# Attention scores as three float32r terms in four 32-row quarters, quartered masks, grouped silus and a new written order

## The reference, cut to what matters

```python
xn = _layernorm(x)                                   # x: 4 batches, 1024 tokens, 128 channels
q, k, v = split(xn @ Wqkv)                           # 16 heads of 8
scores = einsum("bhqd,bhkd->bhqk", rope(Q), rope(K)) / sqrt(8)
attn = softmax(where(causal, scores, min))
y = (attn @ V) @ Wproj
mlp = (silu(xn @ Wg + bg) * (xn @ Wu + bu)) @ Wd + bd
# experts: 4 heads, sums of two lists of top 8 of 64 keys, the best 8 of the sums, softmax of them;
# weight = silu(xn . down_embed[i]) * softmax; states = sum of weight * up_embed[i] over 512 experts
return x + y + mlp + states
```

## Time and profile before

| | us |
|---|---|
| median of 3 runs (lowest, highest) | 736.49 (734.74, 736.72) |
| span of the profiled execution | 737.5 |
| PE busy | 658.8 |
| DVE busy | 591.9 |
| ACT busy | 539.6 |
| POOL busy | 446.4 |

### The profile page before, as it was taken

How to read it: one execution, slowest core, us unless ns; L and a number is a source line. 1 busy time by engine, 2 the same in 40 slices (tenths; PEclk the granted TensorE clock), 3 DMA queues, 4 the chain that set the end, 5 groups by cost and what they waited for, 6 DMA issues and landing times. The chain is left out here.

```text
span 737.5 us, 15130 instructions
## 1 busy us (share of the span) xinstructions
PE 658.8 (89%) x5628; PEld 268.0 (36%) x5628; DVE 591.9 (80%) x1204; ACT 539.6 (73%) x833; POOL 446.4 (61%) x652
## 2 busy tenths in 40 slices
PE   3977787779999989999999979999998999999996
PEld 2433233223334433333234434433333333344343
DVE  4549898999989999896976898877999898855451
ACT  3333455777878676899887686788689999888882
...
GB/s 145 103 127 49 73 36 24 47 14 3 2 14 20 54 74 61 15 71 20 1 10 21 17 80 63 21 76 13 2 14 31 4 14 1 16 32 16 8 15 38
DMA packets 36566, 26.67 MB, mean 36 GB/s; under 512 B 7084, under 2 KB 34092, under 8 KB 36492
## 3 DMA queue, kind: packets, MB, share of 16 engines
...
...
## 5 line engine op out<-in xcount | busy, mean ns | idle before, releaser
L1159 DVE TENSOR_REDUCE pmax<-banks 128x2 f32<-128x1024 f32 (+3 forms) x304 | 342.2, 1160 | 55.6 <-PE banks L1331 36.3
L1006 ACT ACTIVATE pT<-banks 128x1024 f32<-128x1024 f32 (+3 forms) x384 | 295.8, 810 | 74.1 <-PE banks L1359 54.7
L1373 PE MATMUL ybank<-pT,vaug 128*32 128x512 f32 (+3 forms) x1536 | 164.7, 512 | 2.0 <-ACT pT L1006 1.3
L870 POOL TENSOR_TENSOR ssum<-sim 128x512 f32<-128x512 f32 x128 | 145.6, 1143 | 22.9 <-DVE wsum L1206 18.8
L1350 PE MATMUL banks<-qs,ks 51*128 51x512 bf16 (+3 forms) x768 | 123.2, 336 | 22.8 <-ACT pT L1006 14.1
L1321 PE MATMUL banks<-ks,qs 48*128 48x512 bf16 (+3 forms) x768 | 113.4, 337 | 25.5 <-DVE pmax L1159 16.2
L1206 DVE SCALAR_TENSOR_TENSOR wsum<-ssum,best,wsum 128x512 f32<-128x512 f32 x128 | 125.2, 992 | 11.8 <-ACT wsum L1052 11.7
L1052 ACT ACTIVATE wsum<-ssum,wbias 128x512 f32<-128x512 f32 x128 | 90.3, 723 | 24.4 <-POOL ssum L870 22.2
L887 POOL TENSOR_TENSOR coef<-coef,wsum 128x512 f32<-128x512 f32 x64 | 85.4, 1334 | 20.9 <-DVE wsum L1206 20.5
L1350 PEld LDWEIGHTS banks<-qs,ks 51*128 51x128 bf16 x768 | 36.8, 94 | 133.0 <-ACT pT L1006 78.3
L1321 PEld LDWEIGHTS banks<-ks,qs 48*128 48x128 bf16 x768 | 33.1, 94 | 121.6 <-DVE pmax L1159 62.3
...
## 6 DMA issues: line engine op xcount, KB each, us to landing
...
```

Source lines behind the costliest of these rows:

```text
L870: g.tensor_tensor(ssum[:, m % NSS, :, :], s[:, h, 0:XI].unsqueeze(2).to_broadcast([P, XI, NKEYS]), s[:, RH + h:RH + h + 1, :].to_broadcast ...
L1006: a_.activation(pT[:, q % NPT, 2 * e:2 * e + 2, q0:CHUNK], pair(("sc", *n))[:, :, q0:CHUNK], ACT.Exp, scale=SCALE).then_inc(out_sem, 1)
L1159: v.tensor_reduce(pmax[:, c, i % TPC, k0 // CHUNK, js[0] // PP, :, js[0] % PP:js[-1] % PP + 1], pair(("mx", b, c, k))[:, :, 0:wd_ * len(js ...
L1373: ins = t_.matmul(ybank[32 * j:32 * j + 32, q0:CHUNK], vaug[:, b % 2, kt, v0:v0 + 32], pT[:, q % NPT, j, q0:CHUNK], start=kt == 0, stop=kt ...
```

## The change

- **Parts.** A score is now a product in float32r of two parts: `high` (a copy on ACT as float32r, `c0`) and the rest in float32 (`r1` on POOL, `v1` on DVE), which goes into `tAB[:, s, 1, :]`. `c1`, `p2` and `v2` are gone. Three terms remain, so 24 rows a head (26 with the maximum, which has two parts; `n1` has two POOL instructions in place of four). `high` and `tAB` are read by the row DMAs, so `rp` of a unit now waits until the rows of the unit two before have landed, where it waited for `p2` or `v2`.
- **Quarters.** Four heads lie in four 32-row quarters of the array, named by `tile_position`. A score task takes two quarters, and its last number says which two (rows 0 to 63 or 64 to 127). The number of score tasks and of score products is the same.
- **Masks** take four steps of 32 rows (128, 96, 64 and 32 columns for each block in `mx`, 32 to 128 in `sc`) in place of two, still in bf16. The small products grow from 704 to 1408 in `mx` and from 1024 to 2048 in `sc`.
- **Pairs.** "+" in `PE_ORDER` issues two score tasks together, both products first and then their masks in turn. There are 71 such pairs, all of opposite halves, 59 of them of two diagonal tasks; 55 stand behind the last value product of batch 0.
- **DMAs.** The row DMAs are as many as before (12 a unit) with rows of 2 KB in place of 1 KB; those of the maxima go from 32 to 64, those of the rows of ones from 4 to 8.
- **Order.** All five strings are new. The silus of gate and down product of a chunk stand together on ACT, and expert work of the first stages stands further ahead. In the second half of batch 0 the four gate products of its second chunk (`gt.0.1.*`) hold the banks 2 to 5 while 25 score tasks in a row go through the pair 01.

```diff
 TPC = CHUNK // P
 NF = F // P
-PAIRS = H // 2
-GROUPS = H // 4
+ROWS = 32
+NE = P // ROWS
+GROUPS = H // NE
...
-PP = PAIRS // PARTS
-
-TERMS = [(0, 0), (0, 1), (1, 0), (0, 2), (1, 1), (2, 0)]
+PP = GROUPS // PARTS
+
+TERMS = [(0, 0), (0, 1), (1, 0)]
 KQ = len(TERMS) * DH
-KE = KQ + 3
+KE = KQ + 2
...
-            units += [(i, k0, w, range(j, j + n)) for j in range(0, PAIRS, n)]
+            units += [(i, k0, w, range(j, j + n), half) for j in range(0, GROUPS, n) for half in range(2)]
     return sorted(units, key=lambda u: u[3][0] // PP)
...
 
-    order, place = [], {}
+    order, place, partner = [], {}, {}
     for word in text.split():
...
+        together = []
+        for part in word.split("+"):
+            name, _, slot = part.partition("@")
+            kind, *rest = name.split(".")
+            task = (kind, *(int(r) for r in rest))
+            together.append(task)
+            if slot:
+                place[task] = [int(k) for k in slot]
+        order += together
+        if len(together) == 2:
+            partner[together[0]] = together[1]
+    return order, place, partner
...
-qk.0.1.1@45 gt.0.0.3@5 gt.0.0.0@4 up.0.0.1@1 up.0.0.0@4 up.0.0.3@0 xt.1@12 up.0.0.2@6 dn.0.0.2@5 mx.0.0.0@01
+qk.0.1.1@23 dn.0.0.3@6 dn.0.0.0@0 dn.0.0.1@4 vm.1@56 qk.1.0.0@01 mx.0.0.0@23 mx.0.0.1@45 ac.0.0.0@6 mx.0.0.2@23
+sc.3.0.2.3.0@23 sc.3.0.3.0.1@01 pv.3.0.2.2 pv.3.0.2.3 sc.3.0.3.1.1@23+sc.3.0.3.0.0@45 sc.3.0.3.1.0@01 sc.3.0.3.2.0@45
...
 
         ident = sb("ident", [P, P])
-        identb = sb("identb", [P, P], BF16)
-
-        id2 = sb("id2", [P, 2, P], BF16)
-        mask2 = sb("mask2", [P, 2, 1, P], BF16)
-        maskT2 = sb("maskT2", [P, 2, P], BF16)
+
+        shifted = sb("shifted", [P, 2 * P - ROWS], BF16)
+        mask = sb("mask", [P, 1, P], BF16)
+        maskT = sb("maskT", [P, P], BF16)
...
-        parts = sb("parts", [P, 2, 3, CHUNK], BF16)
-        qs = sb("qs", [P, NQS, PAIRS, CHUNK], BF16)
-        ks = sb("ks", [P, 2, PAIRS, T], BF16)
+        high = sb("high", [P, 2, CHUNK], F32R)
+        qs = sb("qs", [P, NQS, GROUPS, CHUNK], F32R)
+        ks = sb("ks", [P, 2, GROUPS, T], F32R)
         VW = (H - 1) * (DH + 1) + 32
...
-                        for hh in range(2 if m > 0 else 1):
-                            r = HALF * hh + DH * t
+                        for e in range(NE if m > 0 else NE // 2):
+                            r = ROWS * e + DH * t
                             dst = ks[r:r + DH, b % 2, :, cols] if a else qs[r:r + DH, m % NQS, :, :]
-                            sp.dma_start(dst, parts[HALF * hh:HALF * (hh + 1), u % 2, term[a], :])\
+                            src = high[:, u % 2, :].bitcast(F32) if term[a] == 0 else tAB[:, u % 2, 1, :]
+                            sp.dma_start(dst.bitcast(F32), src[ROWS * e:ROWS * (e + 1), :])\
                                 .then_inc(rows_loaded[u % 2], 16)
...
-                    g.tensor_tensor(tAB[:, s, 0, :], tAB[:, s, 0, :], parts[:, s, 0, :], ALU.subtract)\
-                        .then_inc(out_sem, 1)
-                elif kind == "p2":
-                    b, c, a = n
-                    s = unit(b, c, a) % 2
-                    w.wait_ge(done["r1"], rank("r1", b, c, a))
-                    w.wait_ge(done["c1"], rank("c1", b, c, a))
-                    g.tensor_tensor(parts[:, s, 2, :], tAB[:, s, 0, :], parts[:, s, 1, :], ALU.subtract)\
+                    g.tensor_tensor(tAB[:, s, 1, :], tAB[:, s, 0, :], high[:, s, :].bitcast(F32), ALU.subtract)\
...
-                    k = mark(g.tensor_tensor(m, m, nparts[:, c, :, h, :, 0, :], ALU.subtract))
-                    need(k)
-                    k = mark(g.tensor_copy(nparts[:, c, :, h, :, 1, :], m))
-                    need(k)
-                    g.tensor_tensor(nparts[:, c, :, h, :, 2, :], m, nparts[:, c, :, h, :, 1, :], ALU.subtract)\
-                        .then_inc(out_sem, 1)
+                    g.tensor_tensor(nparts[:, c, :, h, :, 1, :], m, nparts[:, c, :, h, :, 0, :].bitcast(F32),
+                                    ALU.subtract).then_inc(out_sem, 1)
...
-                    elif u < 2:
-                        w.wait_ge(done["v1"], rank("v1", b, c, a))
-                    else:
-                        w.wait_ge(done["r1"], rank("r1", b, c, a))
-                    a_.activation(parts[:, s, int(kind == "c1"), :], tAB[:, s, 0, :], ACT.Copy).then_inc(out_sem, 1)
+                        w.wait_ge(rows_loaded[a], rows(*unit_at(u - 2)))
+                    a_.activation(high[:, s, :], tAB[:, s, 0, :], ACT.Copy).then_inc(out_sem, 1)
...
-                    v.tensor_tensor(tAB[:, a, 0, :], tAB[:, a, 0, :], parts[:, a, 0, :], ALU.subtract)\
-                        .then_inc(out_sem, 1)
-                elif kind == "v2":
-                    b, c, a = n
-                    w.wait_ge(done["c1"], rank("c1", b, c, a))
-                    v.tensor_tensor(parts[:, a, 2, :], tAB[:, a, 0, :], parts[:, a, 1, :], ALU.subtract)\
+                    v.tensor_tensor(tAB[:, a, 1, :], tAB[:, a, 0, :], high[:, a, :].bitcast(F32), ALU.subtract)\
                         .then_inc(out_sem, 1)
...
-                    if u >= 4:
-                        w.wait_ge(done["p2"], rank("p2", *unit_at(u - 2)))
-                    elif u >= 2:
-                        w.wait_ge(done["v2"], rank("v2", *unit_at(u - 2)))
+                    if u >= 2:
+                        w.wait_ge(rows_loaded[a], rows(*unit_at(u - 2)))
                     v.tensor_tensor(tAB[:, u % 2, :, :], pair(("qk", b, c, a)), cs[:, :, c * CHUNK:(c + 1) * CHUNK],
                                     ALU.mult).then_inc(out_sem, 1)
...
+            def quarter_masked(task, h):
+
+                kind, b, c, *n = task
+                if kind == "mx":
+                    i, k0, wd_, js, half = MAX_UNITS[c][n[0]]
+                    m = P - ROWS * h
+                    for e in range(2):
+                        r = slice(ROWS * (2 * half + e), ROWS * (2 * half + e + 1))
+                        blocks = pair(task)[:, e, 0:len(js) * wd_].rearrange("p (j w) -> p j w", w=wd_)
+                        ins = t_.matmul(blocks[:, :, wd_ - m:wd_], shifted[r, m - ROWS:m - ROWS + P],
+                                        mask[r, :, 0:m].to_broadcast([ROWS, len(js), m]), start=False,
+                                        stop=h == NE - 1, skip_group_check=True, tile_position=(r.start, 0))
+                else:
+                    gr, kt, half = n
+                    q0 = first_column(c, kt)
+                    m = ROWS * (h + 1)
+                    for e in range(2):
+                        r = slice(ROWS * (2 * half + e), ROWS * (2 * half + e + 1))
+                        ins = t_.matmul(pair(task)[:, e, q0:q0 + m], shifted[r, P - m:2 * P - m],
+                                        maskT[r, P - m:P], start=False, stop=h == NE - 1,
+                                        tile_position=(r.start, 0))
+                if h == NE - 1:
...
+                    for s, j in enumerate(js):
+                        for e in range(2):
+                            q = ROWS * (2 * half + e)
+                            r = slice(q, q + KQ)
+                            ins = t_.matmul(pair(task)[:, e, s * wd_:(s + 1) * wd_],
+                                            qs[r, serial(b, c) % NQS, j, i % TPC * P:(i % TPC + 1) * P],
+                                            ks[r, b % 2, j, k0:k0 + wd_], start=s == 0,
+                                            stop=not diagonal(task) and s == len(js) - 1, skip_group_check=True,
+                                            tile_position=(q, 0))
+                    if not diagonal(task):
+                        ins.then_inc(done["mx"], 1)
...
+                for e in range(2):
+                    q = ROWS * (2 * half + e)
+                    r = slice(q, q + KE)
+                    ins = t_.matmul(pair(task)[:, e, q0:CHUNK], ks[r, b % 2, gr, kt * P:(kt + 1) * P],
+                                    qs[r, serial(b, c) % NQS, gr, q0:CHUNK], start=True, stop=kt < c * TPC,
+                                    tile_position=(q, 0))
+                if not diagonal(task):
+                    ins.then_inc(done["sc"], 1)
...
-                elif kind == "mx":
...
-
-                        for h in range(2):
-                            for e in range(2):
-                                r = slice(HALF * e, HALF * (e + 1))
-                                blocks = bank[:, e, 0:len(js) * wd_].rearrange("p (j w) -> p j w", w=wd_)
-                                ins = t_.matmul(blocks[:, :, wd_ - P + HALF * h:wd_], id2[r, h, :],
-                                                mask2[r, h, :, HALF * h:].to_broadcast([HALF, len(js), P - HALF * h]),
-                                                start=False, stop=h == 1, skip_group_check=True)
...
+                elif kind in ("mx", "sc"):
+                    if task not in PARTNER.values():
```

(13 more changed lines are left out.)

803 lines of the change are left out of this document (396 added, 407 removed), and 5 rows, old and new, of the table KINDS.

## The result

| | before | after |
|---|---|---|
| median, us (lowest, highest; runs) | 735.89 (734.74, 736.72; 4) | 888.56 (878.61, 889.75; 4) |
| ratio, 95% interval | | 1.205 (1.198 to 1.211) |
| span of the profiled execution | 737.5 | 886.9 |

The changed kernel is 153 us slower. 729 had been predicted, within 708 to 770. First the page of the changed kernel, which answers the earlier trace rows, and the busy times by stage, cut where the same work ends as in the earlier trace rows: the first max scores (55 us, before 48), the last output copy of batch 0 (338, before 256), the last one of all (867, before 716).

What follows compares the result with a forecast made beforehand. VectorE was taken to bound the stage to batch 0's last copy, TensorE the next. 268 + 439 + 22.8 = 729.8 us, less 1.0 from profiled execution to median, gave 729; own range 708 to 734, stated range 708 to 770.

Steps and rivals of the forecast that it cites:

- Score products, "as many, with as many columns": TensorE's float32r score products: same number and columns, at bf16's price, 0.23 us for 512 columns through both halves.
- the rival of half the rate: TensorE's score products: float32r at half of bf16's rate, about 86 us added in TensorE's stage, 815 us; chance 0.05.
- the rival of the types: Float32r scores beside bf16 masks: 0.09 us per type change, 45 us, time 774; chance 0.14, weight loads included.
- 404 us of TensorE's work: Stage from 256 to 716 us of the old kernel: 404 us of TensorE's work and 56 us of waits.
- The quarters: Behind batch 0: ScalarE some 31 us less work, TensorE 18 us more for masks (range 18 to 27).
- The masks' term: Four mask steps on TensorE: 0.06 to 0.09 us more per diagonal task, 18 to 27 us behind batch 0.
- Work moved ahead: Expert work put before batch 0's last copy: VectorE 21 us more there, 21 less behind; copy at 268, before 256.
- One pair of banks: First stage: 25 score tasks sharing pair 01 go in turn, 7 to 11 us more, 740 us; chance 0.06.
- The waits: TensorE's stage behind batch 0: 31 us of 56 us of waits remain, stage 439 us; bounds 15 to 56.
- Pairs: Two score tasks at once behind batch 0: 55 pairs give 6 us, between nothing and 16.
- the tail: Products behind the last value product: two more products, four transposes less, 22.8 us where it was 21.5.
- The first stage: Before the first max score: 4 us later, between nothing and 8, so the first product at 51 us.

Runs made afterwards that it cites:

- e2: The changed kernel with its two parts, queries and keys in bf16 instead of float32 and float32r, row DMAs carrying half the bytes: 795.81 us, ratio 1.080 to the kernel before.
- e9: The changed kernel with the free rows of each quarter filled with zeros, to 30 and 32 rows: 864.05 us, ratio 1.176 to the kernel before.
- e8: Old code under the new strings, gate products `gt.0.1.*` moved behind the 25 score tasks, which take three bank pairs in turn: 803.16 us, against 798.54 without the move.

## Why the prediction was wrong, step by step

Of the 153 us the type has 93, by two pairs of runs. The other 60 come with strings and quarters together; each of them costs about as much alone, and why they do not add is open.

- **Score products, "as many, with as many columns" at bf16's price: the step that failed most.** Half of it was right. Float32r streams at bf16's rate (128 columns in 0.07 us, above); the rival of half the rate is gone. That fits what the prediction took from the Trainium skill's FP8 and Floating Point Precision, section TensorE Precision Notes, where a reduced FP32 is read cut to fewer bits and only true FP32 takes four passes. But I costed the products and not their weight loads: the 0.23 us from a product of 512 columns to its masks came out at 0.34. At 0.10 to 0.12 us (0.18 to 0.20 at the lower clock, at which a third of the loads run) 688 tasks (384 of `sc`, 304 of `mx`) come to 86 to 100 us as an estimate, less where two tasks go as a pair or a load runs under a product of its own task. The runs have 93 to 96, and 82 to 90 of them behind the first score product. (That it is the loads is read from the records, from the same addition at every length, and from the ten steps with the load ahead, which lack it; no run took a load away by itself.) "Weight loads of four bytes an element that don't hide" stood as half a sentence in the rival of the types, whose price was taken from a change of type. Of that price there is nothing, neither into the masks (the ten steps) nor out of them (0.14 us to the next score, 0.16 in e2).
- The Trainium skill, TensorE: Matmul & The Clock Gate, section Weight-path perf modes — Fast Weight Load (FWL) and DoubleRow, says that the fast weight load is on when there are 128 weights and the input isn't FP32. I had not weighed it. The trace agrees in that the 4-byte loads take 214 and 222 ns on the mean, where bf16's take 93 and 96; no run here says whether that mode is the reason.
- **"404 us of TensorE's work"** was carried over from one trace as if a product had one duration. It has it at one clock, and the clock of the earlier trace rows is a result of that kernel: 0.99 in that stage became 0.86. No term of the sum held a clock. What lowered it is not settled: zeros in the free rows bring it to 0.95 and the time down by 25 us (e9), and the bf16 parts with the same 48 to 52 rows have 0.92 there (e2).
- **The quarters** were to bring 30 us of ACT's work and take 18 to 27 of masks behind batch 0. The masks' term was about right in size: 0.05 to 0.07 us more for a diagonal task, by the runs, where 0.06 to 0.09 was forecast. A step of 32 columns takes 40 ns (30 in e2), one of 64 takes 28 and one of 96 takes 42, so that 32 columns are no cheaper than 64, which is what the Trainium skill's TensorEngine Tiling (Array Packing), section Instruction Overhead, has; by columns alone they would be. (The 2 us that the prediction put on it come out at 3 to 4 by its own price of a column, 28 of them for 295 tasks.) The whole was not right: +79 under the old strings. 22 to 30 of these are masks as an estimate (432 tasks by 0.05 to 0.07); the rest goes with a clock of 0.88 for 0.97, whose cause in the quarters isn't settled.
- **Work moved ahead.** I summed durations: 12 us later at batch 0, 21 us sooner behind. With the new code the strings give 19 to 23 us, so the sign was right there; with the old code the same strings cost 62, which no sum of durations shows. The last copy of batch 0 came at 338 instead of 268; of these 70 us the type has 40 (e2: 298), and 11 of the 40 are there ahead of the first score.
- **One pair of banks** was named as a rival of 7 to 11 us: e8 shows nothing of it, though only with the old code.
- **The waits.** 439 us of TensorE's stage rested on 31 us of waits left. They fell from 118 to 103 us in the rows, but a stage of 529 us is 506 busy: the waits weren't the question any more.
- **Pairs** (6 us), **table loads** (19) and **the tail** (22.8; it was 19.6) were of the right size, or too small to be told.
- **The first stage** had the right mechanism at the wrong end of its range: 4 us of 0 to 8 were taken, and the first product came at 55.4 us, 8 late, not at 51. The wait for the first rows alone was 5.5 us on VectorE.
